# A two-layer graph kernel: first norm in quarters, weights turned on TensorE, maxima through TensorE, first tiles split apart, and the first layer's sums taken out by ScalarE

## What is computed

```python
h = relu(layernorm(x))                       # first norm
# layer 0: two attention steps on the same adjacency, then an MLP
for i in range(2):
    Wh = h_i @ W[i]
    u, v, c = Wh @ L1 @ a, Wh @ L2 @ a, lb @ a
    e = leaky_relu(u + v.T + c, 0.2)
    att = softmax(where(adj > 0, e, -9e15), axis=1)
    h_{i+1} = 0.2 * h + 0.8 * elu(att @ Wh)
x = x + concat([h, h_1, h_2]) @ mlp_w + mlp_b
# layer 1: mean over the neighbours
h = relu(layernorm(x))
x = x + concat([a @ h / deg, h]) @ weight + bias
```

## Time and profile before

| | |
|---|---|
| median of 3 runs | 1882.42 us (1879.76 to 1882.54) |
| the profiled execution's own time | 1880.38 us |
| its span, first to last instruction | 1878.6 us |
| busy: TensorE, VectorE, ScalarE, GpSimd | 1552.6, 1598.8, 1230.0, 147.3 us |
| moved by DMA | 353.91 MB, 188 GB/s over the span |
| mean granted TensorE clock | 0.955 of full |

### The profile page before, as it was taken

How to read it: one execution, slowest core, us unless ns; L and a number is a source line. 1 busy time by engine, 2 the same in 40 slices (tenths; PEclk the granted TensorE clock), 3 DMA queues, 4 the chain that set the end, 5 groups by cost and what they waited for, 6 DMA issues and landing times. The chain is left out here.

```text
span 1878.6 us, 50382 instructions
## 1 busy us (share of the span) xinstructions
PE 1552.6 (83%) x21780; PEld 1500.3 (80%) x21780; DVE 1598.8 (85%) x2697; ACT 1230.0 (65%) x1269; POOL 147.3 (8%) x162
## 2 busy tenths in 40 slices
PE   0223788888888888888874999999999999899998
PEld 0122777877878787878764999999999999889998
DVE  1669999999999999999986976886977968987675
ACT  0335576878877787778856899999999999000000
POOL 0017100000000000000005100000000000000000
PEclk9956889999999999999986999999999999999999
DMA  7128789999999999999921111111212101133231
GB/s 192 56 46 297 280 319 353 380 354 373 376 366 388 360 384 353 397 347 409 343 91 23 52 53 35 52 42 58 58 39 66 53 24 52 41 86 109 85 97 48
DMA packets 130912, 353.91 MB, mean 188 GB/s; under 512 B 25217, under 2 KB 33409, under 8 KB 130689
## 3 DMA queue, kind: packets, MB, share of 16 engines
q1 hardware_dynamic: 90240, 304.10, 43.6%
q0 software_dynamic: 7936, 25.24, 5.4%
q10 hardware_dynamic: 32512, 21.34, 3.9%
HBM read 323.32 MB, written 27.33 MB: 187 GB/s over the span
## 5 line engine op out<-in xcount | busy, mean ns | idle before, releaser
L462 ACT ACTIVATE region<-ub,bigv 128x1024 uint8<-128x1024 f32 x1024 | 1098.2, 1142 | 54.7 <-PE bank L1312 22.1
L1312 PE MATMUL bank<-wsplit,region 128*128 128x195 bf16 x8192 | 789.1, 250 | 86.3 <-DVE region L706 47.2
L1312 PEld LDWEIGHTS bank<-wsplit,region 128*128 128x128 fp8e3 x8192 | 692.0, 99 | 103.5 <-issue 47.9
L1318 PE MATMUL bank<-wsplit,region 128*128 128x130 f16 x8192 | 564.4, 223 | 66.3 <-DVE region L714 65.4
L1318 PEld LDWEIGHTS bank<-wsplit,region 128*128 128x128 fp8e3 x8192 | 505.8, 99 | 96.4 <-DVE region L714 94.8
L714 DVE SCALAR_TENSOR_TENSOR region<-region 128x512 uint32<-128x512 uint32 x512 | 347.1, 695 | 24.1 <-PE bank L1318 23.4
L706 DVE SCALAR_TENSOR_TENSOR region<-region 128x512 uint32<-128x512 uint32 x512 | 343.4, 699 | 1.4 <-ACT region L462 1.3
L726 DVE TENSOR_SCALAR region<-region 128x4096 uint8<-128x4096 int32 x128 | 294.4, 2301 | 0.9 <-DMA region<-in_adj 0.8
L1506 PE MATMUL bank<-wsplit,region 128*128 128x129 f16 x4096 | 242.9, 221 | 11.4 <-DVE region L1148 11.4
L1506 PEld LDWEIGHTS bank<-wsplit,region 128*128 128x128 fp8e3 x4096 | 240.7, 98 | 12.8 <-DVE region L1148 12.8
L470 ACT ACTIVATE region<-bank 128x1024 uint16<-128x1024 uint16 x64 | 65.3, 1021 | 134.0 <-PE bank L1302 133.4
(11 more groups left out here) (156 smaller groups left out, 775.7 us busy)
## 6 DMA issues: line engine op xcount, KB each, us to landing
region<-in_adj SPq DMA_DIRECT2D x128, 2048.0 KB, 10.9
region<-codes_d SPq DMA_DIRECT2D x128, 256.0 KB, 2.7
codes_d<-region ACTq DMA_DIRECT2D x64, 256.0 KB, 5.9
ub<-u_d POOLq DMA_DIRECT2D x16, 512.0 KB, 5.0
hg<-h_d POOLq DMA_DIRECT2D x16, 256.0 KB, 5.3
region<-in_x SPq DMA_DIRECT2D x8, 256.0 KB, 5.5
h_d<-hg ACTq DMA_DIRECT2D x8, 256.0 KB, 2.0
x_d<-region POOLq DMA_DIRECT2D x8, 256.0 KB, 4.7
```

The source lines that it names most:

```text
L462: last = nc.scalar.activation(sv[:, b, :], ub[G % 2][:, :], ACT.Relu, bias=bigv[l][:, t:t + 1], scale=BIG)
L1312: return nc.tensor.matmul(acc_on[it], columns(onb[U % NS], it, b), wsplit[:, c * TC + 2 * q + b, 0:WC], start=(c == 0 and q == 0 and b == ...
L1318: return nc.tensor.matmul(acc_off[it], columns(offb[U % NO], it, b), woff[:, c * TC + 2 * q + b, WO:WO + WF], start=(c == 0 and q == 0 and ...
```

## The change

It has six parts, and the lists of the engines are rewritten around them.

1. x is loaded in four quarters. The first norm is done on quarters, with one root over all 64 columns of row sums. It runs on C·x minus the row sum, which saves the division. The result stands in the memory that later holds the split parts. h0 is stored unscaled (GpSimd's queue), and the factor ALPHA moves into `hq` and `residual`. The MLP's bias is added in the second layer (`old_x`).
2. All weight loads move to SyncE's queue behind x and lose their element-wise ones; W is turned on TensorE, and the two attention vectors are made by a multiplication and a sum on VectorE.
3. The three maxima over partitions go through TensorE (`spread_max`, `max_row`, `max_out`) in place of GpSimd.
4. v, u and x0 of the first products are read by VectorE straight from PSUM (`columns_0`); ScalarE takes only Wh.
5. The first two tiles of both sides are split by VectorE alone (`split_first`), and TensorE may begin its first unit with these; the conversions of the first one and a half chunks stand between the columns.
6. In the first layer, for groups 0 to 6, ScalarE takes the sums out of PSUM, scaled (`scaled_sums`: 16 instructions), and VectorE adds the parts (`add_pairs`, `add_third`) in place of `sums_out` and `row_scales`. The row work of the group before, and its turning and products, come up to one chunk earlier. In the gap between the layers four masks stand ahead of `sums_out`.

```diff
@@ sync
-                for k in range(NG):
-                    sp.dma_start(pairs(xr[:, grp(k), :]), x_v[k]).then_inc(x_in[k], 16)
+                for k in range(4):
+                    sp.dma_start(pairs(xr[:, quarter(k), :]), x_v[k]).then_inc(x_in[k], 16)
+                for hf in range(2):
...
+                            sp.dma_start(lin[:, :, k, :], lin_w[:, C * (1 - k):C * (2 - k), :].rearrange("l c h -> c l h")).then_inc(wts, 16)
...
@@ gpsimd
-                pool.wait_ge(wmx_s, 2)
-                nc.gpsimd.partition_all_reduce(wmx[:, 1, :], wmx[:, 0, :], P, RMAX).then_inc(w_max, 1)
...
+                for k in range(4):
+                    pool.wait_ge(hn_r, k + 1)
+                    pool.dma_start(h0_d.rearrange("p (t c) -> p t c", c=C)[:, quarter(k), :], hn[:, quarter(k), :]).then_inc(h0_st, 16)
                 for k in range(NG):
                     store_u(k)
                     if k < 2:
                         load_u(k)
-                    pool.wait_ge(x0_r, k + 1)
+                    pool.wait_ge(x0_r, 3 * k + 3)
                     pool.dma_start(dgrp(x0_d, k), xr[:, grp(k), :]).then_inc(x0_st, 16)
-                pool.wait_ge(vm, 1)
-                nc.gpsimd.partition_all_reduce(hmx[:, 1, :], hmx[:, 0, :], P, RMAX).then_inc(vall, 1)
@@ scalar
-                for l in range(2):
-                    act.dma_start(wt[:, l, :], w[l].rearrange("c o -> o c"), allow_slow_non_contiguous=True).then_inc(wts, 16)
-                    act.dma_start(lwt[:, l, :], lin_w[l].rearrange("c h -> h c"), allow_slow_non_contiguous=True).then_inc(wts, 16)
...
+                def scaled_sums(e):
+                    if e > 0:
+                        act.wait_ge(red, e)
+                    for it in range(IT):
+                        if it % 2 == 0:
+                            act.wait_ge(on_sum, 4 * e + it // 2 + 1)
+                        t = IT * e + it
+                        nc.scalar.activation(part5[:, it, 0:3, :], acc_on[it].rearrange("p (j c) -> p j c", c=CE), ACT.Copy,
+                                             scale=rowf[:, t, 0:1]).then_inc(on_out[0], 1)
...
+                for k in range(NG + 1):
                     if k < NG:
-                        high(k)
-                        h0_scaled(k)
-                    if 1 <= k < NG + 1:
-                        take_ht(k - 1, bank[6 + (k - 1) % 2])
-                    if k >= 2:
+                        take_ht(k, bank[6 + k % 2])
+                    if k >= 1:
                         for r in range(3):
-                            products(k - 2, r, bank[3 * (k % 2) + r])
+                            products(k - 1, r, bank[3 * ((k - 1) % 2) + r])
+                ramps(0, 0, 0)
                 exps(0)
...
                     ramps(0, n, 3)
-                    if g > 1 and r < 3:
-                        products(NG + g - 2, r, tpb)
-                    if g > 0 and r == 4:
+                    if g > 0 and r == 7:
+                        products(NG + g - 1, 0, tpb)
+                    if g > 1 and r < 2:
+                        products(NG + g - 2, r + 1, tpb)
+                    if g > 0 and r == 0:
+                        scaled_sums(g - 1)
+                    if g > 0 and r == 3:
                         row_exp(g - 1)
@@ vector
+                def columns_0(k, r):
...
+                    nc.vector.tensor_scalar(vu[:, :, t0:t0 + nt].rearrange("p s t -> p t s"), pv[:, :, C:C + 2], winv, None,
+                                            ALU.mult).then_inc(u_r, 1)
+                    nc.vector.scalar_tensor_tensor(xr[:, t0:t0 + nt, :], pv[:, :, C + 2:], winv, xr[:, t0:t0 + nt, :],
+                                                   ALU.mult, ALU.add).then_inc(x0_r, 1)
...
+                def max_row(n):
+                    dve.wait_ge(mx_t, n + 1)
+                    wc.mark(nc.vector.tensor_reduce(mxr[:, :], bank[3][0:2, 0:P], AX.X, ALU.max))
+                    wc.sync()
+                    nc.vector.tensor_scalar(diag[:, :], identf[0:2, 0:2], mxr[:, 0:1], None, ALU.mult).then_inc(mx_d, 1)
...
+                def add_pairs(e):
+                    dve.wait_ge(on_out[0], IT * (e + 1))
+                    dve.wait_ge(off_out[0], IT * (e + 1))
...
+                    ec.mark(nc.vector.tensor_tensor(av[:, :, :], part5[:, :, 0, :], part5[:, :, 1, :], ALU.add))
+                    ec.mark(nc.vector.tensor_tensor(bb[:, :, :], part5[:, :, 3, :], part5[:, :, 4, :], ALU.add))
+
+                def add_third(e):
+                    ec.sync()
+                    nc.vector.tensor_tensor(av[:, :, :], av[:, :, :], part5[:, :, 2, :], ALU.add).then_inc(red, 1)
...
+                for k in range(4):
+                    centre(k)
+                attention_vectors()
+                variance(0)
+                variance(1)
+                w_turned()
+                variance(2)
+                variance(3)
...
+                for k in range(NG):
+                    for r in range(3):
+                        columns_0(k, r)
+                    if k > 0:
+                        largest_0(k - 1)
+                    if k == 1:
+                        convert(0, 0)
+                    if k == 2:
+                        convert(0, 1)
+                        pack_pairs(0)
+                    if k == 3:
+                        pack(0)
+                    if k == 5:
+                        convert(1, 0)
+                biased_0()
+                largest_0(NG - 1)
                 max_parts(0)
-                convert(0, 0)
-                convert(0, 1)
-                pack_pairs(0)
+                convert(1, 1)
+                max_row(1)
+                pack_pairs(1)
+                max_out(1, hmx[:, 1, :])
                 scales(0)
-                pack(0)
-                convert(1, 0)
+                pack(1)
                 scales_end(0)
+                split_first(0)
                 split_on(0, 0)
@@ tensor
+                def spread_max(n, src):
+                    nc.tensor.transpose(bank[3][0:2, 0:P], src, identf[:, :]).then_inc(mx_t, 1)
+                    pe.wait_ge(mx_d, n + 1)
+                    nc.tensor.matmul(bank[3][:, P:P + 2], ones2[:, :], diag[:, :], start=True, stop=True).then_inc(mx_b, 1)
```

More of the change, by code:

```diff
@@ L495, in _ @@
                     g, r = n // NCH, n % NCH
-                    ramps(0, n, 0)
+                    if n > 0:
+                        ramps(0, n, 0)
                     ramps(0, n, 1)
                     take_codes(n)
-                    if r == 6 and g > 0:
+                    if r == 5 and g > 0:
                         high(NG + g - 1)
@@ L684, in scales_end, with split_first @@
                     nc.vector.tensor_scalar(rowf[:, :, 1], rowf[:, :, 1], hsc[:, 3:4], None, ALU.mult).then_inc(scl, 1)
+                def split_first(l):
+                    on, off = expv[:, 0:2, 0:1].to_broadcast([P, 2, CE]), expv[:, 0:2, 1:2].to_broadcast([P, 2, CE])
+                    part = [wsplit[:, 0:2, j * CE:(j + 1) * CE] for j in range(3)]
+                    hi, lo = woff[:, 0:2, WO:WO + CE], woff[:, 0:2, WO + CE:WO + WF]
+                    full, rest, small = av[:, 0:2, :], bb[:, 0:2, :], po[:, 0:2, :]
+                    dve.wait_ge(scl, l + 1)
+                    if l == 0:
+                        dve.wait_ge(tT, NG)
+                        dve.wait_ge(h0_st, 16 * 4)
+                    else:
+                        dve.wait_ge(on_sum, 4 * NG)
+                        dve.wait_ge(off_sum, 3 * NG)
+                        dve.wait_ge(w_on, NCH)
+                        dve.wait_ge(w_off, NCH)
+                    ec.sync()
+                    sc.mark(nc.vector.tensor_tensor(full, hw[:, 0:2, :], on, ALU.mult))
+                    sc.mark(nc.vector.tensor_tensor(small, hw[:, 0:2, :], off, ALU.mult))
+                    sc.sync()
+                    sc.mark(nc.vector.tensor_copy(part[0], full))
+                    sc.mark(nc.vector.tensor_copy(hi, small))
+                    sc.sync()
+                    sc.mark(nc.vector.tensor_tensor(rest, full, part[0], ALU.subtract))
+                    nc.vector.tensor_tensor(lo, small, hi, ALU.subtract).then_inc(w_first, 1)
+                    sc.sync()
+                    sc.step(nc.vector.tensor_copy(part[1], rest))
+                    nc.vector.tensor_tensor(part[2], rest, part[1], ALU.subtract).then_inc(w_first, 1)
@@ L821, in _ @@
-                for k in range(NG + 2):
-                    if k + 1 < NG:
-                        centre(k + 1)
-                    if 1 <= k < NG + 1:
-                        low(k - 1)
-                    if k < NG:
-                        normal(k)
-                    if k == 0:
-                        weights()
-                        weights_split()
-                    if k >= 2:
-                        columns_out(k - 2)
+                for k in range(4):
+                    centre(k)
@@ new lines, in _ @@
+                normal(2)
+                low0(1)
```

(11 more changed lines are left out.)

493 lines of the change are left out of this document (275 added, 218 removed).

## The result

The changed kernel takes 1793.24 us (median of four runs, 1788.33 to 1794.82) against 1881.81 us for the kernel before beside it: ratio 0.9527, 95% interval 0.9506 to 0.9547, so 4.7% less. That is faster, as I said, but 21 us slower than the 1772 I predicted and 1.2 us above the upper end of my range.

What follows compares the result with a forecast made beforehand. VectorE was taken to bound the first layer, TensorE the second layer and mean stage, with waiting chains at the start and between layers. 1880.4 - 83 - 17 - 9.5 + 0.5 = 1771.4, stated as 1772 us, range 1757 to 1792.

Steps and rivals of the forecast that it cites:

- part 1: Start of the kernel, before the first mask: first mask at 78 us instead of 161, -83 us (-87 to -71).
- A second hold: Start: VectorE's fourth conversion would hold the last x0 store until 64 us, without it 62; moves the sum by 2 us.
- VectorE's own list: Start: VectorE's steps from centring and norm through columns, maxima, conversion and scales, forecast to end at 69 us.
- rival (a): Start gives less through x0 store wait, port and TensorE's banks: first mask at 90, total 1784 us; chance 0.14.
- Part 2: First layer, VectorE full: 2.55 us saved at each of seven group borders, -17 us in all (-18 to -9).
- The +1 for loads: First layer: charge for adjacency loads near their DMA limit, +1 us for all borders (0 to +8).
- Rivals (b) to (f): Loads bind 1789 (0.1); more gained 1761 (0.14); ScalarE bound 1790 to 1840 (0.04); ScalarE order 1888 (0.02); start bound otherwise 1855 (0.01).
- Part 3: Gap between the layers: shorter maximum and earlier masks, partly given back at TensorE's next dry spell, -9.5 us (-16 to -5).
- Parts 4 and 5: Second layer and mean stage, bound by TensorE: small additions mostly hidden, +0.5 us (0 to +2).

Runs made afterwards that it cites:

- The run with the held load: Changed kernel with SyncE's fifth adjacency load of half a chunk, and all behind it, held until x0 is stored whole: 1780.86 us.
- the versions without the wait: Changed kernel with u in 32-byte runs reordered by the ramps and exponentials first, 1771.5 us; also with a semaphore per x0 store and first tiles split whole, 1769.89 us.
- the run that undoes it: Changed kernel with VectorE again reducing and scaling the sums out of PSUM at the first layer's borders: 1809.61 us, ratio 0.962.
- the run with whole tiles: Changed kernel with the first chunk's eight tiles split whole by VectorE and GpSimd in both layers, TensorE waiting for all: 1788.04 us.

## Why the prediction was wrong in its number and right in its shape

**The step that failed** is in part 1: "The last store is issued at 62 to 64 and lands 5 to 9 us later". It was issued at 71.75 and landed at 91.9, 19.6 us after its issue was over. I named the chain that would end last (exponentials behind ramps, ramps behind the store of x0, VectorE waiting) and gave it the wrong size: VectorE waited 20.07 us where I had allowed 0.5 to 6.5. Two things went into that, the landing and the issue.

The landing. I bounded it by rows of the kernel before, where eight stores are spread from 75.9 to 142.5 us. Its windows from 76 to 143 us have the DMA engines 0.21 to 0.41 busy. In the changed kernel eight stores of x0, eight of u, two loads of u and the adjacency meet within 24 us. I counted one load of the adjacency in flight in place of two and left the stores of u out of the sum without a reason. The run with 32-byte runs shows that they are a cause: landing 7.5 us in place of 16.0, inside the 5 to 9 that I had given, and a time of 1773.59. That this time is so near to 1772 is in part luck: its first mask is 4 us later than forecast, and the first layer gained 3 us more. The run with the held load (8.2 us) shows that the adjacency is the other ingredient: with either one taken away the stores land nearly as I had bounded them.

The issue. I let GpSimd's stores go out as soon as the columns are done. GpSimd's queue stood 10.17 us at the second load of u, which waits until u is stored, and the stores behind it went out late. My sum had no term for this. A second hold was in the prediction and occurred: the issue of a store at 67.48 took 2.24 us in place of 0.54, beside VectorE's fourth conversion. Moving the second load of u behind the stores gives 7.6 us.

**VectorE's own list** came to 74.4, not 69. The columns begin at 41.2 (39.5), 1.19 of it a wait for ScalarE. They and the maxima take 25.6 us (22.5): a group takes 1.90 us and not 1.76, the second one waits 1.35 more for ScalarE, and the rest are small steps between them that I had not listed. From there it is 7.6 (7). Small terms of one sign, 5.4 us in all. The sum had allowed 2.5 us of waiting for the exponentials (69 to 71.5); less these, some 3 us stay of the miss in the versions without the wait, whose first mask is at 81, not 78.

**The last step of the sum** doesn't follow either: it comes to 1771.4 for a profiled execution, and with the 2 us by which the text puts the median above it, to 1773.4 and not 1772. Measured against 1773.4 the miss is still 20 us.

**My rival (a)** named the mechanism, "the ramps' wait for the stored x0", and priced it at a first mask of 90. It is 101.7. The direction was covered by my range, the size was not; the range for the landing had no bound from a row in which the engines were full.

**Part 2** held: -20.3 for -17, though it lies 2 us outside its own range (-18 to -9). The border gives 2.52 by the run that undoes it, the forecast said 2.55. The +1 for loads wasn't needed; beyond the 17.6 us some 2.7 came from the rest of the part (the earlier row work, the loads or VectorE's waits). Which of these is not told apart. At a border ScalarE follows TensorE bank by bank as described:

```profile
510.73 0.74 ACT L496 ACTIVATE parts<-bank,rowf 128x195 f32<-128x195 f32 x2 [2.74 <-PE bank L1445]
...
515.04 2.19 ACT L502 ACTIVATE parts<-bank,rowf 128x130 f32<-128x130 f32 x8
...
517.07 4.31 ACT L475 ACTIVATE region<-ub,bigv 128x1024 uint8<-128x1024 f32 x4
...
527.70 0.69 DVE L849 TENSOR_TENSOR av<-parts 128x520 f32<-128x520 f32 x1
528.31 0.69 DVE L850 TENSOR_TENSOR bb<-parts 128x520 f32<-128x520 f32 x1
```

The last sum is out at 517.2, ten microseconds before VectorE adds, and no ramp came late: over this layer VectorE's conversions show 0.1 us of idle time before them where the earlier trace rows have 0.9 for the same operation. Rivals (b) to (f) did not occur. The DMA share of 0.97 at 369 GB/s is no bound, since VectorE is 199.83 of 200 us busy beside it.

**Part 3** held: -8.4 for -9.5. The step from partial to whole maximum:

```profile
909.75 0.22 DVE L706 TENSOR_REDUCE hmx<-vu 128x1 f32<-128x64 f32 x1
...
911.99 0.16 DVE L715 TENSOR_TENSOR cv<-hmx,cb 128x1 f32<-128x1 f32 x1
...
917.30 2.77 PE L1445 MATMUL bank<-wsplit,region 128*128 128x195 bf16 x16 [5.54 <-issue]
...
946.42 1.54 PE L1445 MATMUL bank<-wsplit,region 128*128 128x195 bf16 x16 [2.61 <-DVE region L791]
```

2.2 us, where the earlier trace rows have 10.8 (forecast 1.7). Of the 15.3 us that TensorE's first product comes earlier, 6.95 are lost again by the third chunk, as I said; the run with whole tiles adds that it costs a little net. **Parts 4 and 5**: -0.1 for +0.5, too little to tell from nothing.

## What to carry to other kernels

A change that squeezes a loose start makes transfers meet that were apart. So the landing time of a store must be taken from a row in which the DMA engines are as full as they will be, and everything that the queues carry in that stretch counts, also what the change doesn't touch. Where DMA engines are full at a low rate, look for the transfer with the shortest run in DRAM, however few its bytes: here that was the cause. And a wait for all of a set of stores, where each user needs one of them, costs nothing until the last is late: here a semaphore per store removed the same 20 us as the cure of the landing.

## What the runs showed of the hardware that I had not expected

Six stores of u of 4 KB each, in runs of 8 bytes, cost about 11 us of all sixteen DMA engines (the estimate above), nearly all of it in the 4 KB packets of other transfers, and a 256 KB store beside them lands in 16.0 us instead of 7.5 (medians). The Trainium skill (DMA: Bandwidth & Descriptors, Specifications) asks for transfers of at least 512 B for the full rate, and has the engines read, modify and write below that. Both patterns are below it, and the packets under 512 B are as many (377 and 379); yet beside runs of 32 bytes the rate stays near 415 GB/s and beside those of 8 it breaks down, which the page's threshold alone doesn't tell.

VectorE is slower while GpSimd splits. In the changed kernel, second layer, the same operations beside GpSimd's splitting (which ends at 947.3) and after it:

```profile
922.91 1.26 DVE L782 CAST wsplit<-av 128x520 bf16<-128x520 f32 x1
...
930.39 3.10 DVE L799 SCALAR_TENSOR_TENSOR region<-region 128x512 uint32<-128x512 uint32 x2
...
952.27 0.43 DVE L782 CAST wsplit<-av 128x520 bf16<-128x520 f32 x1
...
955.76 1.29 DVE L799 SCALAR_TENSOR_TENSOR region<-region 128x512 uint32<-128x512 uint32 x2
```

The cast takes 1.26 us in place of 0.43 and two off masks 3.10 in place of 1.29. The Trainium skill (SBUF — State Buffer, Terms, "shared port pair") calls the port pair that VectorE and GpSimd share an exclusive lock, held for a whole instruction; operations that take two or three times as long beside GpSimd agree with it. The run with the exponentials first points the same way: it moved GpSimd's splitting 20 to 25 us ahead but the first mask only 6, and VectorE then went through the same list from the first to the ninth on mask in 32.75 us instead of 42.55. A run in which GpSimd stands still during the masks wasn't made, and the DMA traffic differs there too, so that the port is the reason is argued from these rows and not shown by an experiment.
